# The message layer's rows turned before the weights, and the mixed heads turned by TensorE: one edit of a four-layer graph network kernel

## The reference

```
L0: h = X @ W (256 -> 128); alpha = softmax(leaky_relu(self_i + neigh_j) + mask); out = [alpha @ h, h]
L1: mi = x @ Wi.T; mj = x @ Wj.T; deg = adj.sum(axis=1)
    out = deg[:, None] * (mi + b) + adj @ mj
L2: 8 heads of 32: softmax(q k.T / sqrt(32), masked) @ v, then @ Wo.T + bo
L3: Wh = x @ W (256 -> 256); alpha = softmax(leaky_relu(src_i + dst_j), masked); out = alpha @ Wh
```

## Time and profile before

| | |
|---|---|
| time, median of 3 runs | 1175.25 us (1173.5 to 1176.16) |
| profiled execution, its own time | 1172.01 us |
| its span, first to last instruction | 1170.2 us |
| granted TensorE clock, mean over the span | 0.981 of full |
| ACT busy | 1087.6 us (93%) |
| PE busy, modelled | 1089.8 us (93%) |
| DVE busy | 1050.3 us (90%) |
| POOL busy | 957.3 us (82%) |

### The profile page before, as it was taken

One profiled execution on the slowest core, in us unless ns is written; L12 is line 12 of the kernel. 1 busy time (PEld: TensorE's weight loads), 2 busy tenths in 40 slices (PEclk: granted clock), 3 DMA queues, 4 the chain that ended last, 5 costly groups with the idle time before them and its releaser, 6 DMA issues.

```text
span 1170.2 us, 39812 instructions
## 1 busy us (share of the span) xinstructions
PE 1089.8 (93%) x15256; PEld 917.1 (78%) x15256; DVE 1050.3 (90%) x2975; ACT 1087.6 (93%) x3209; POOL 957.3 (82%) x1734
## 2 busy tenths in 40 slices
PE   3689999999999999999999999999999999999865
PEld 3577888888888888888888888888888888888752
DVE  4489999999999999999999999999999999999861
ACT  3589999999999999999999999999999999999862
POOL 3789888888888888888888888888888888887521
PEclk9899999999999999999999999999999999999895
DMA  5258998889888989888998889889889978997761
GB/s 146 46 108 134 163 171 157 143 166 167 149 153 164 164 147 154 163 164 133 173 163 153 152 164 164 136 164 167 159 141 167 160 149 153 168 163 127 133 129 48
DMA packets 575933, 173.33 MB, mean 148 GB/s; under 512 B 539648, under 2 KB 575744, under 8 KB 575744
## 3 DMA queue, kind: packets, MB, share of 16 engines
q1 hardware_dynamic: 574976, 170.46, 80.8%
q10 hardware_dynamic: 768, 0.33, 0.1%
HBM read 19.73 MB, written 16.78 MB: 31 GB/s over the span
## 4 chain that ended last, share of the span: by engine, by line
ACT 52%; PE 22%; DMA 13%; DVE 5%; POOL 4%; issue 2%; SPq 0%; DVEq 0%; POOLq 0%
DMA h_t<-h_rows 8%; PE ps L399 5%; PE ps L401 5%; PE ps L400 5%; ACT ps L1059 4%; DMA mix_t<-mix_rows 3%; ACT ps L1065 3%; ACT ps L1071 3%; ACT ps L1076 2%; ACT relu L1107 2%; ACT relu L977 2%; ACT relu L980 2%; ACT head_hi L1081 2%; ACT agg_hi L1035 2%; ACT relu L1104 2%
## 5 line engine op out<-in xcount | busy, mean ns | idle before, releaser
L399 PE MATMUL ps<-w_hi,h_t 128*128 128x258 f16 (+2 forms) x768 | 188.8, 258 | 28.1 <-DMA h_t<-h_rows 26.0
L401 PE MATMUL ps<-w_hi,h_t 128*128 128x258 f16 (+2 forms) x768 | 188.2, 257 | 0.0
L400 PE MATMUL ps<-w_lo,h_t 128*128 128x258 f16 (+2 forms) x768 | 188.1, 256 | 0.0
L399 PE MATMUL ps<-w_hi,agg_hi 128*128 128x256 f16 x512 | 139.1, 272 | 1.8 <-DVE agg_lo L783 1.8
L401 PE MATMUL ps<-h_t,w_lo 128*128 128x256 f16 x512 | 139.6, 273 | 0.0
L400 PE MATMUL ps<-h_t,w_hi 128*128 128x256 f16 x512 | 139.6, 273 | 0.0
L399 PE MATMUL ps<-h_t,w_hi 128*128 128x256 f16 x512 | 139.6, 273 | 0.0
L401 PE MATMUL ps<-w_hi,agg_lo 128*128 128x256 f16 x512 | 138.8, 271 | 0.0
L400 PE MATMUL ps<-w_lo,agg_hi 128*128 128x256 f16 x512 | 138.8, 271 | 0.0
L399 PEld LDWEIGHTS ps<-w_hi,h_t 128*128 128x128 f16 x768 | 75.4, 98 | 44.6 <-DMA h_t<-h_rows 31.6
L399 PE MATMUL ps<-v_hi,head_t_hi 128*128 128x33 f16 x1024 | 84.6, 178 | 11.1 <-issue 10.5
(11 more groups left out here) (189 smaller groups left out, 5052.4 us busy)
## 6 DMA issues: line engine op xcount, KB each, us to landing
x<-in_x SPq DMA_DIRECT2D x64, 256.0 KB, 3.2
out<-x SPq DMA_DIRECT2D x64, 256.0 KB, 2.3
h_t<-h_rows SPq DMA_TRANSPOSE x192, 3.6
head_t_hi<-head_hi SPq DMA_TRANSPOSE x64, 5.1
head_t_lo<-head_lo SPq DMA_TRANSPOSE x64, 4.4
mix_t<-mix_rows SPq DMA_TRANSPOSE x64, 3.1
w_f<-in_w_o SPq DMA_DIRECT2D x1, 256.0 KB, 3.3
w3t_f<-in_w_t SPq DMA_DIRECT2D x1, 256.0 KB, 3.5
```

The costliest lines, as they stand in the source:

```text
L399: pe.matmul(o, lh, rh, start=start, stop=False)
L400: pe.matmul(o, lh, rl, start=False, stop=False)
L401: return pe.matmul(o, ll, rh, start=False, stop=stop)
```

## The change

In the message layer the split rows are written side by side (`h1_rows`) and turned by a DMA transpose (`move1`, new on SP) to `h1_t`. `message_source` multiplies them with Wj, `message_own` with Wi, 12 matmuls of 256 columns each. Only the neighbours' part is copied to fp16 (`keep_message`, 512 columns for both graphs) and its remainder taken (`split_message`); `gather` multiplies it with the adjacency as the stationary operand, two matmuls of 512 columns. `update1_own` adds the own part times the degree, `update1` the gathered part.

In the attention layer `head_norm` writes fp32 rows to SBUF (`heads`); four fp32 transposes on PE (`turn_out_0/1`) turn them into one bank; `keep_out` and `split_out` (512 columns each) make `out_hi` and `out_lo`, which `project_0/1` use. `move_out` is gone.

The banks are dealt out anew and the lists of all five engines are in a new order; some pieces move to another part (`move2` and `norm2_0` from 3 to 4, `head_norm` and the split of the output from 5 to 6, `stats1` from 1 to 2, `head_max_3` and the exponentials of head bank 0 from 4 to 5, `keep_value` and `split_value` from 5 to 4).

```
-            def aggregate(bank, hi, lo, b):
-                for c in range(KC):
-                    o = bank[:, c * 2 * P:(c + 1) * 2 * P]
-                    pe.matmul(o, hi[:, b, c * P:(c + 1) * P], agg_deg[:, :], start=True, stop=False)
-                    last = pe.matmul(o, lo[:, b, c * P:(c + 1) * P], agg_deg[:, :], start=False, stop=True)
-                return last
...
+            def move1(g):
+                sp.wait_ge(relu_lo1_done, g + 1)
+                sp.dma_start(h1_t[g % 2][:, :, :], h1_rows[g % 2][:, :, :, :].rearrange("p h b d -> p (h b d)"), transpose=True).then_inc(move1_done[g % 2], 16)
...
+            def message_source(g):
...
+                pe.wait_ge(move1_done[g % 2], 16 * (g // 2) + 16)
+                for b in range(GROUP):
+                    for c in range(KC):
+                        last = triple(mj_ps[:, b * D:(b + 1) * D], h1_t[g % 2][:, b * KC + c, :], h1_t[g % 2][:, (GROUP + b) * KC + c, :], w_hi[:, c, COL_WJ:COL_WJ + D], w_lo[:, c, COL_WJ:COL_WJ + D],
+                                      start=(c == 0), stop=(c == KC - 1))
+                last.then_inc(message_source_done, 1)
...
+            def gather(g):
+                pe.wait_ge(split_message_done, g + 1)
+                pe.matmul(ag_ps[:, :], agg[:, :], mj_hi[g % 2][:, :], start=True, stop=False)
+                last = pe.matmul(ag_ps[:, :], agg[:, :], mj_lo[g % 2][:, :], start=False, stop=True)
+                last.then_inc(gather_done, 1)
...
+            def turn_out_0(g):
+                pe.wait_ge(head_norm_0_done, g + 1)
+                turn(to_ps, heads[g % 2], 0)
...
+            def turn_out_1(g):
+                pe.wait_ge(head_norm_1_done, g + 1)
+                turn(to_ps, heads[g % 2], 1).then_inc(turn_out_1_done, 1)
...
             def project_0(g):
...
-                pe.wait_ge(move_out_done[g % 2], 16 * (g // 2) + 16)
-                if g < graph_groups - 1:
-                    pe.wait_ge(split_head_0_done, g + 2)
+                pe.wait_ge(split_out_done, g + 1)
...
+            def keep_message(g):
+                act.wait_ge(message_source_done, g + 1)
+                act.activation(mj_hi[g % 2][:, :], mj_ps[:, :], ACT.Copy, scale=UNSCALE).then_inc(keep_message_done, 1)
...
+            def keep_out(g):
+                act.wait_ge(turn_out_1_done, g + 1)
+                act.activation(out_hi[g % 2][:, :], to_ps[:, :], ACT.Copy).then_inc(keep_out_done, 1)
```

More of the change, by code:

```diff
@@ L21 @@
 BANK = 512
-FOLD = [0, 1, 2, 3]
+FOLD = [0, 1, 2, 4]
 EPS = 1e-5
@@ L121, in build @@
         prob_t3 = pair("prob_t3", [P, GROUP * P], F32)
[L123 to L126, removed]
+        h1_rows = pair("h1_rows", [P, 2, GROUP, D], F16)
+        h1_t = pair("h1_t", [P, 2 * GROUP * KC, P], F16)
+        mj_hi = pair("mj_hi", [P, GROUP * D], F16)
+        mj_lo = pair("mj_lo", [P, GROUP * D], F16)
         h2_rows = pair("h2_rows", [P, 2, GROUP, D], F16)
@@ L142, in build @@
         head_inv = pair("head_inv", [P, GROUP, HEADS], F32)
-        mix_rows = pair("mix_rows", [P, 2, GROUP, D], F16)
-        mix_t = pair("mix_t", [P, 2 * GROUP * KC, P], F16)
+        heads = pair("heads", [P, GROUP, D], F32)
+        out_hi = pair("out_hi", [P, KC * GROUP * P], F16)
+        out_lo = pair("out_lo", [P, KC * GROUP * P], F16)
         h3_rows = pair("h3_rows", [P, 2, GROUP, D], F16)
@@ L151, in build @@
         ps = [ctx.enter_context(nc.psum_tensor(f"ps{k}", [P, BANK], F32)) for k in range(BANKS)]
[L152 to L173, removed]
+        f0_ps = ps[3]
+        r0_ps = ps[7]
+        p0_ps = ps[3]
+        s0_ps = ps[2]
+        mj_ps = ps[1]
+        mi_ps = ps[7]
+        ag_ps = ps[1]
+        q_ps = ps[4]
+        k_ps = ps[1]
+        v_ps = ps[7]
+        sc0_ps = ps[5]
+        sc1_ps = ps[6]
+        sc2_ps = ps[4]
+        sc3_ps = ps[0]
+        sh0_ps = ps[2]
+        sh1_ps = ps[7]
+        to_ps = ps[2]
+        pr_ps = ps[2]
+        f30_ps = ps[6]
+        f31_ps = ps[3]
+        r3_ps = ps[2]
+        p3_ps = ps[3]
+        s3_ps = ps[3]
         sc_ps = [sc0_ps, sc1_ps, sc2_ps, sc3_ps]
@@ L221, in build @@
         add_deg_bias_done = sem("add_deg_bias_done")
[L222 to L230, removed]
+        move1_done = [sem(f"move1_done_{k}") for k in range(2)]
+        message_source_done = sem("message_source_done")
+        message_own_done = sem("message_own_done")
+        keep_message_done = sem("keep_message_done")
+        split_message_done = sem("split_message_done")
+        gather_done = sem("gather_done")
+        update1_own_done = sem("update1_own_done")
+        update1_done = sem("update1_done")
         stats2_0_done = sem("stats2_0_done")
@@ L267, in build @@
         head_norm_0_done = sem("head_norm_0_done")
-        head_sum_1_done = sem("head_sum_1_done")
         invert_heads_1_done = sem("invert_heads_1_done")
         head_norm_1_done = sem("head_norm_1_done")
[L271 to L274, removed]
+        turn_out_1_done = sem("turn_out_1_done")
+        keep_out_done = sem("keep_out_done")
+        split_out_done = sem("split_out_done")
         project_1_done = sem("project_1_done")
@@ L376, in slot @@
                 at(0, load_x)
+                at(4, move2)
                 at(7, move3)
@@ L379, in slot @@
                 at(5, move_heads_lo)
-                at(3, move2)
+                at(2, move1)
                 at(0, move0)
-                at(5, move_out)
                 at(7, store_x)
@@ L498, in message_1 @@
                     for c in range(KC):
[L499 to L502, removed]
+                        last = triple(mi_ps[:, b * D:(b + 1) * D], h1_t[g % 2][:, b * KC + c, :], h1_t[g % 2][:, (GROUP + b) * KC + c, :], w_hi[:, c, COL_WI:COL_WI + D], w_lo[:, c, COL_WI:COL_WI + D],
+                                      start=(c == 0), stop=(c == KC - 1))
@@ L640, in slot @@
             def slot(at):
-                at(2, aggregate_0)
-                at(7, logit_rows3)
+                at(4, make_value)
+                at(1, turn_probs0_0)
+                at(1, turn_probs0_1)
+                at(4, head_scores)
                 at(1, gat_sum0)
-                at(4, head_scores)
-                at(5, head_sum_1)
-                at(5, head_sum_0)
-                at(2, message_0)
                 at(7, turn_probs3_0)
                 at(7, turn_probs3_1)
-                at(2, message_1)
+                at(5, head_sum_1)
                 at(7, gat_sum3)
-                at(4, make_value)
-                at(3, make_query)
+                at(5, head_sum_0)
+                at(2, message_source)
                 at(0, feat0)
+                at(5, turn_out_0)
+                at(5, turn_out_1)
+                at(2, message_own)
+                at(2, gather)
                 at(5, project_0)
                 at(5, project_1)
+                at(3, make_query)
+                at(6, feat3_1)
                 at(0, logit_rows0)
+                at(6, feat3_0)
                 at(3, make_key)
-                at(6, feat3_0)
-                at(1, aggregate_1)
-                at(6, feat3_1)
-                at(0, turn_probs0_0)
-                at(0, turn_probs0_1)
+                at(6, logit_rows3)
             run(slot)
@@ L912, in update3_1 @@
+            def update3_1(g):
                 dve.scalar_tensor_tensor(x[g % XBUF][:, 1, :], s3_ps[:, 1 * D:2 * D], inv3[g % 2][:, 1:2], x[g % XBUF][:, 1, :],
-                                         ALU.mult, ALU.add)
+                                         ALU.mult, ALU.add).then_inc(update3_1_done, 1)
             def slot(at):
-                at(3, update1_1)
-                at(3, update1_0)
+                at(2, stats1_0)
+                at(6, head_norm_0)
+                at(6, head_norm_1)
+                at(2, stats1_1)
+                at(5, head_max_3)
+                at(2, mean_var1)
+                at(3, split_message)
+                at(6, split_out)
+                at(5, split_head_2)
+                at(0, stats0_1)
+                at(0, stats0_0)
+                at(5, split_head_1)
+                at(0, mean_var0)
+                at(3, update1_own)
```

328 lines of the change are left out of this document (141 added, 187 removed).

## The result

The changed kernel takes 1204.57 us (median of 4 runs, 1203.07 to 1207.1) against 1174.38 for the kernel before, run beside it: a ratio of 1.026, 95% interval 1.0234 to 1.0285. The forecast was 1154, range 1138 to 1186: wrong, and wrong in sign.

A forecast was written before the change was run, and what follows sets the result against it. ACT was taken to set the slot of 16.93 us; new floors near 16.2 plus 0.2 to 0.5 of waits gave 16.6, so -0.33 x 63 = -21 us from 1175.25: 1154 us, range 1138 to 1186.

The forecast's parts named there:

- what bounded the kernel before: ACT: its list of 16.72 us plus 0.21 of waits set the slot of 16.93.
- the sums of the engines: Work per slot after the change: ACT 16.18 us, PE 16.2, DVE about 16.0, GpSimd unchanged at 14.9.
- The four fp32 turns: New transposes of the mixed heads on PE: 0.48 us a slot from starts alone, 0.58 with the handover.
- One DVE term: `update1_own` on DVE, counted at 0.59 us like the other 512-column operations.
- the rings through SP's queue: Chains returning one slot later through SP's transposes: 16.65 us by the heads' (down to 15.2), about 16.0 by `move1`.
- the ring through `move1`: Chain in which `move1` has to land before `message_source`: about 16.0 us a slot.
- The ring in the slot above: Through `move0` and `feat0`; the prediction only said layer 0's transposes queue behind the heads on SP, without a size.
- the third rival: Late head transposes make the kernel slower: slot 17.35, +26 us, 1201 us; chance 0.18.
- Its ring: From `head_sum_1` to `turn_out_1` on PE, `keep_out` to `keep_head_3` on ACT, heads' transposes, back: 16.65 us.
- Its condition: Heads' hi hold plus lo landing averaging 8.0 us instead of 7.3; at 7.6 the ring equals 16.93.
- the idle queue ahead of the hi transpose: On SP, taken to speak for a hi hold below its 2.90 us median, down to 1.53 (ring 15.2).
- the expected gain: ACT's copies fall by 0.54 us a slot; 0.33 of slot time was to arrive, 21 us in all.

The follow-up runs named there:

- number 12: The kernel before with one more 512-column copy on ACT a slot: 1191.58 us, ratio 1.0159.
- number 9: The kernel before with its heads' transposes issued in two pieces: 1171.6 us, ratio 0.9993.
- number 10: The changed kernel with the heads' transposes in two pieces and one more 512-column copy on ACT: 1177.68 us, ratio 1.004.
- Number 1: The changed kernel with the two turns of the mixed heads ahead of `feat0` on PE: 1191.66 us, ratio 1.0157.
- number 5: The changed kernel with each of the heads' two transposes issued in two pieces, same bytes: 1158.99 us, ratio 0.9879.
- 6: The changed kernel with half of the heads' lo transpose left out: 1162.57 us, ratio 0.991.
- number 13: The changed kernel with `move1` issued for the first two groups only, later groups using those rows: 1182.13 us, ratio 1.0077.
- 3: The changed kernel with `keep_feat0` behind `keep_head_3` on ACT: 1191.63 us, ratio 1.0163.
- number 4: The changed kernel with one more 512-column copy a slot on ACT, behind `keep_head_3`: 1196.42 us, ratio 1.0202.
- number 2: The changed kernel with the two turns of the mixed heads ahead of `message_source` too: 1295.84 us, ratio 1.1057.
- number 11: The changed kernel with `move1` moving 2 of its 8 blocks, used for all: 1199.4 us, ratio 1.0233.

## Why the prediction was wrong

**Right: what bounded the kernel before.** ACT set the slot, with a list of 16.72 us and 0.21 of waits (number 12), and the heads' transposes had slack (number 9).

**Right: the sums of the engines.** ACT's new list starts one instruction behind another from `keep_out` at 511.37 to the end of `keep_head_2` at 527.74, 16.37 us with small waits in it; the forecast was 16.18. The four fp32 turns take 0.44 to 0.46 in all, not 0.58. One DVE term was too small: `update1_own`, which takes its factor from a column (`deg_unscale`), starts 0.71 ahead of its successor, not 0.59. The rows (DVE timeline, then PE's):

```profile
514.61 0.72 DVE L787 SCALAR_TENSOR_TENSOR x<-ps,deg_unscale,x 128x512 f32<-128x512 f32 x1
515.32 0.69 DVE L836 TENSOR_TENSOR head_lo<-ps,head_hi 128x512 f16<-128x512 f32 x1
...
510.73 0.60 PE L392 MATMUL ps<-ident,heads 128*128 128x128 f32 x4
511.17 0.27 PE L397 MATMUL ps<-w_hi,h_t 128*128 128x256 f16 x1
```

With the ring loosened the work shows itself as cheaper: 16.76 a slot and 1159 us, close to the forecast of 16.6 and 1154, and ACT's room is then small (number 10).

**Wrong: the rings through SP's queue.** The step that failed is the sentence that gives the ring through `move1` "by the same sums about 16.0". Number 1 shows 17.40 for it, 10.4 of them from the issue of the hi transpose to the landing. The ring in the slot above closes one transfer later, through `move0` and `feat0`, which I had named as queued there and not followed. The prediction has no term for the landing of a transpose queued behind the heads': layer 0's rows landed 2.8 us after their issue before the change (median), 4.2 after it, and 4.76 in the slot shown. From `keep_head_3` to the landing it took 2.76 + 2.72 + 1.31 + 4.76 and the handovers, 11.7 us; with ACT's 4.42 and PE's 1.38 this is 17.50.

That the holds of SP's queue lengthen the slot is shown by taking pieces out: half of the heads' queue time (numbers 5 and 6) and `move1`'s issue (13). That it is this ring is read from the chain; the gains of numbers 1 and 3 fit it, but other rings stand close behind. One of them the prediction doesn't have at all: `move2` now stands behind `store_x`, which waits for the end of DVE's list. By the chains it is about 17 us long and likely belongs to the floor in numbers 1, 5 and 13. No run moves `move2` or `store_x`, so this is read from traces and not tested.

**Half right: the third rival.** It named the heads' transposes as the cause of a slow version, gave 1201 us, and had a chance of 0.18. Its ring, which closes through `head_sum_1` and needs neither `move1` nor `move0`, is likely one of two at the floor of 17.03 in number 13, beside the one through `store_x`; this is argued from the waits, and not tested alone. Its condition, a hi hold and lo landing of 8.0 us together, is met in single slots (in the changed kernel 413.12 to `head_sum_1` at 421.08) but not by the medians, 1.93 + 4.9 = 6.8. That its 1201 lies so close to the result is luck in part, since other rings stood in the chain too. What I got wrong in weighing it was to count the idle queue ahead of the hi transpose as relief. The hi hold did fall (median 2.90 before, 1.93 after), but the lo hold rose from 2.13 to 2.53 and its landing from 4.4 to 4.9.

**Where the expected gain went.** 0.54 us of ACT's work a slot did go. It could not arrive, since the slot was no longer ACT's sum; the waits on the rings took its place and cost 0.50 more. Before, `move_out` was issued behind `move0`; the transpose that replaces it stands between the heads' and `move0`. Of the 50 us between forecast and result, 46 come back with the heads' two pieces, and 22 with the message rows' issue alone; the two overlap.

**Open.** Why one more copy off the ring made the changed kernel 8 us faster (number 4); how much of the slot the ring through `store_x` sets; and the rest of the loss in number 2. The two halves of the change were not built each by itself on the old lists.

## What to carry to other kernels

In a pipeline of in-order engines, add up the rings as carefully as the engines: follow each transfer that stands behind a late one in the issuing queue to the work that it feeds, and back. A queue that idles while its first input is half ready can be a gain: issue what is ready, in pieces. Look also for what is ready and stands behind an issue that waits. Work taken off the busiest engine pays only down to the longest ring, so compute that length before counting the saving.

## What the runs showed of the hardware

A transpose of 2 blocks of 128 columns held SP's queue as long as one of 8 (1.63 and 1.66 us median), while pieces of 8 blocks, cut from one of 16, held it 1.33 us where the whole held it 1.93 to 2.53. So below 8 blocks a smaller transfer did not make the queue faster. What stands ahead counts too: `move1` whole held 1.66 us behind the heads' lo transpose of 16 blocks and 1.34 behind a piece of 8 (number 5). Splitting both cost 4 x 1.33 - 1.93 - 2.53 = 0.9 us more hold in all. A full DMA share (1.01 over 11.7 us) was not what set the time in the slot shown: at 0.76 the same stretch took 11.6 us in number 11. And one more 512-column copy on ACT cost 19 us in two kernels and -8 us in a third.
